# A five-stage audio tower on one core: layernorm applied by ScalarE, and new orders for all engines

## The chip, the core and the metric

The kernel runs on one core of one Trainium2 chip. Its engines run side by side and meet only at semaphores: TensorE (PE in the profile; its weight loads are PEld), VectorE (DVE), ScalarE (ACT), GpSimd (POOL) and SyncE (SP), which here only issues DMAs. The metric is the device time of one launch in microseconds (us), the median of several runs.

## What is computed

The input is 64 sequences of 256 frames of 80 channels. The reference, cut to what matters here:

```python
h = relu(taps5(x) @ W + b)                          # 252 positions of 128 features per sequence
h = batchnorm(h)                                    # statistics over ALL sequences and positions
h = h + attention0(layernorm(h))                    # 8 heads, softmax, band added to the scores
h = h + moe0(layernorm(h))                          # 8 experts of 256, gelu, top 2 of the gates
h = h + linear_attention1(layernorm(h))             # causal, 8 heads, elu + 1
h = h + moe1(attention2(layernorm(layernorm(h))))   # second layernorm has gain and bias; 2 heads, causal;
                                                    # 8 experts of 512, all gates used

def _layernorm(x, axis=-1, eps=1e-05):
    m = jnp.mean(x, axis=axis, keepdims=True)
    v = jnp.var(x, axis=axis, keepdims=True)
    return (x - m) / jnp.sqrt(v + eps)
```

So after the batch norm there are four layernorms per sequence. (The fourth is two in a row, which the kernel folds into one by another variance offset.)

## The kernel before

**Phase 1** (to about 165 us) works on pairs of sequences, 504 positions at a time: `load_x`, a transpose (`turn_input`), the five taps (`taps`), relu on ScalarE, statistics on VectorE, and the result goes to DRAM (`store_y`). Two pairs make a double step k (0 to 15). Beside it the weights arrive in eight pieces of 128 x 1906 float32 (`load_piece`); each is split into a high and a low float16 half by ScalarE (`high_of_piece`) and VectorE (`low_of_piece`). Pieces 0 and 1 come first, piece i+2 in the double step 2i (`PIECE_AT`).

**Phase 2** does everything else for 32 pairs p. Products of float32 values are made from three float16 matmuls (`mm3`: high x high, high x low, low x high). Five kinds of work are written as generators, each cut into steps that end at a `yield`; every engine has its own version of each:

- q, 7 steps: batch norm of pair p, transpose, layernorm, projections of attention 0; their float16 terms go to DRAM and come back spread over partitions (SP's `load_terms`)
- a, 32 steps: attention 0, its output projection, the second layernorm, the gates of the first experts
- l, 48 steps: the third layernorm, linear attention 1, the fourth layernorm, causal attention 2, the gates of the second experts
- h, 48 a round: `hidden`, one chunk of 128 hidden features: PE 3 matmuls of 504 columns into `pf`, ScalarE gelu with bias (L859), VectorE a cast to the high half (L1247), GpSimd the low half (L652)
- o, 48 a round: `output`, one chunk back to 128 features: PE 12 matmuls of 128 columns; at the last chunk of an expert VectorE adds the gated sum to h in four instructions (L1266), and the next expert's first chunk on PE waits for that (`gated`)

The order of the work is written out by hand: one string of 183 letters for each engine and round (`PE_ROUND` and so on), with others for the start and the end. A letter takes the next step of that kind. All engines are in-order, so a step that waits holds up all behind it on its engine. In round r, a belongs to pair r+1, l to pair r, q to pair r+2; the first 28 h belong to the second experts of pair r-1, the next 16 to the first experts of pair r+1.

A layernorm is: `norm_stats` on VectorE (bn_stats L932, bn_aggr L936, variance plus eps L940), `norm` on GpSimd (power -1/2, L584), `norm_apply` on VectorE (L948, four instructions of 126 x 128, minus the mean, times rstd), then `turn` on PE (four transposes, L1327), `high` on ScalarE (L706) and `low` on VectorE (L954).

In the code, PE steps are numbered from 0 in each kind: the layernorm transposes are q5, a24, l2 and l28; the projections of attention 0 are q6 (L1282 to L1284 into pa); its first scores are a0 (L1390, they wait for the spread terms); the logits of the first gates are a25, the transpose of the gates is a29 (L1342) and the product with the output biases a30 (L1348, it waits for ScalarE's copy `gate_t`, L715).

## Time and profile before

| | |
|---|---|
| runs, us | 4356.4, 4362.26, 4363.68 (median 4362.26) |
| profiled execution, us | 4363.7, its span 4362.0 |
| mean granted TensorE clock | 0.982 of 2.4 GHz |
| busy: PE, PEld | 4059.1 us (93%), 2996.2 us (69%) |
| busy: DVE, ACT, POOL | 3341.9 (77%), 2669.0 (61%), 2539.1 (58%) |

PE's busy time is the union of matmuls in flight. A matmul of 128 columns is shown as 0.22 us long but the next one starts 0.06 us later, so PE can lose some time between two that the busy share does not show.

### The profile page before, as it was taken

To read this page: it belongs to the slowest core of one execution; us is meant where nothing else is said; L and a number is where in the kernel's file an instruction comes from. 1 tells how busy PE (TensorE), PEld (TensorE's weight loads), DVE (VectorE), ACT (ScalarE), POOL (GpSimd) and SP (SyncE) were. 2 spreads that over 40 slices of the span, in tenths; PEclk is the share of its full clock that TensorE was granted. 3 is DMA by queue.
4 is the path that set the end of the run, shared out by engine and by line. 5 is a ranking of instruction groups with operands and counts; after the bars stand their busy time and mean duration, and the time that the engine had idled before them with its cause. 6 is when DMAs were issued, how large, how long until landed. Compare 5 with 4: busy or idle time off the path is not lost.

```text
span 4362.0 us, 104576 instructions
## 1 busy us (share of the span) xinstructions
PE 4059.1 (93%) x41344; PEld 2996.2 (69%) x41344; DVE 3341.9 (77%) x9262; ACT 2669.0 (61%) x4345; POOL 2539.1 (58%) x2366
## 2 busy tenths in 40 slices
PE   7678999999999999999999999999999999999998
PEld 3346777776777777677777767777777777777666
DVE  3367777877887777788777778878777887777776
ACT  3235666666666666666666666666666666666654
POOL 2134666666666666666656665665666566666655
PEclk9779999999999999999999999999999999999999
DMA  4200000101100010110001011000101100010000
GB/s 143 72 27 27 20 18 26 30 28 30 30 23 18 23 30 28 30 30 25 20 19 30 28 30 30 28 20 16 30 28 30 30 27 19 18 30 28 28 16 6
DMA packets 136937, 127.60 MB, mean 29 GB/s; under 512 B 28928, under 2 KB 135360, under 8 KB 136448
## 3 DMA queue, kind: packets, MB, share of 16 engines
q1 hardware_dynamic: 136448, 120.91, 9.5%
q8 instruction: 328, 5.37, 0.5%
q14 instruction: 161, 1.32, 0.1%
HBM read 71.05 MB, written 49.55 MB: 28 GB/s over the span
## 4 chain that ended last, share of the span: by engine, by line
PE 53%; DVE 25%; ACT 6%; POOL 5%; issue 4%; DMA 4%; SPq 3%; ACTq 0%; DVEq 0%
PE pf L1282 8%; PE pa L1542 8%; PE pf L1284 7%; PE pf L1283 7%; DVE hid_hi L1247 5%; DVE h L1266 5%; PE pa L1428 3%; PE pa L1524 3%; DMA qk_spread<-terms 3%; PE pa L1414 2%; PE pa L1390 2%; PE pa L1282 2%; PE pa L1622 2%; POOL inv_norm L642 2%; SPq L462 2%
## 5 line engine op out<-in xcount | busy, mean ns | idle before, releaser
L652 POOL TENSOR_TENSOR hid_lo<-hid,hid_hi 128x504 f16<-128x504 f32 x1536 | 1836.6, 1210 | 1363.0 <-DVE hid_hi L1247 1363.0
L859 ACT ACTIVATE hid<-pf,vec 128x504 f32<-128x504 f32 x1536 | 1030.6, 681 | 704.1 <-PE pf L1284 547.1
L1282 PE MATMUL pf<-w_hi,hid_hi 128*126 128x128 f16 x6144 | 1133.4, 224 | 46.0 <-DVE h L1266 45.2
L1284 PE MATMUL pf<-w_hi,hid_lo 128*126 128x128 f16 x6144 | 1119.3, 222 | 0.0
L1283 PE MATMUL pf<-w_lo,hid_hi 128*126 128x128 f16 x6144 | 1119.2, 222 | 0.0
L1282 PEld LDWEIGHTS pf<-w_hi,hid_hi 128*126 128x126 f16 x6144 | 846.6, 138 | 187.0 <-DVE h L1266 88.3
L1283 PEld LDWEIGHTS pf<-w_lo,hid_hi 128*126 128x126 f16 x6144 | 847.5, 138 | 40.3 <-issue 1.4
L1284 PEld LDWEIGHTS pf<-w_hi,hid_lo 128*126 128x126 f16 x6144 | 849.1, 138 | 0.0
L1247 DVE CAST hid_hi<-hid 128x504 f16<-128x504 f32 x1536 | 708.3, 486 | 24.1 <-ACT hid L859 23.9
L1266 DVE SCALAR_TENSOR_TENSOR h<-pf,gates,h 126x128 f32<-126x128 f32 x2048 | 572.8, 341 | 78.0 <-PE pf L1284 77.7
L1282 PE MATMUL pf<-xf_hi,w_hi 128*128 128x504 f16 x1536 | 582.3, 379 | 3.7 <-DVE xf_lo L1229 1.5
L1284 PE MATMUL pf<-xf_hi,w_lo 128*128 128x504 f16 x1536 | 580.8, 378 | 0.0
L1283 PE MATMUL pf<-xf_lo,w_hi 128*128 128x504 f16 x1536 | 580.3, 378 | 0.0
L608 POOL TENSOR_TENSOR pt<-pt,band 126x262 f32<-126x262 f32 x512 | 345.0, 698 | 135.8 <-ACT pt L751 133.8
L1542 PE MATMUL pa<-v,pt 126*126 126x65 f32 x3072 | 382.5, 274 | 1.6 <-DVE o L1147 1.2
L751 ACT ACTIVATE pt<-pa 126x504 f32<-126x504 f32 x512 | 274.5, 588 | 157.6 <-PE pa L1414 156.6
L1542 PEld LDWEIGHTS pa<-v,pt 126*126 126x126 f32 x3072 | 360.9, 191 | 2.1 <-issue 2.1
L1047 DVE TENSOR_REDUCE minus_max<-pa 126x2 f16<-126x504 f32 x512 | 325.9, 682 | 45.8 <-PE pa L1390 44.8
L859 ACT ACT_TABLE_LOAD x248 | 318.2, 1283 | 4.4
L1157 DVE TENSOR_TENSOR pt<-pa,causal 126x504 f32<-126x504 f32 x256 | 173.2, 676 | 151.8 <-PE pa L1524 151.8
L1284 PEld LDWEIGHTS pf<-xf_hi,w_lo 128*128 128x128 f16 x1536 | 150.4, 98 | 179.4 <-issue 4.2
L706 ACT ACTIVATE ot_hi<-pa 128x504 f16<-128x504 f32 x192 | 113.3, 590 | 253.1 <-PE pa L1327 253.0
(206 smaller groups left out, 7390.0 us busy)
## 6 DMA issues: line engine op xcount, KB each, us to landing
qk_spread<-terms SPq DMA_DIRECT2D x224, 126.0 KB, 2.5
qk_spread<-terms SPq DMA_DIRECT2D x192, 63.0 KB, 2.3
y_scratch<-hid SPq DMA_DIRECT2D x32, 252.0 KB, 2.1
y_in<-y_scratch SPq DMA_DIRECT2D x32, 252.0 KB, 3.4
terms<-qk_hi SPq DMA_DIRECT2D x32, 252.0 KB, 2.5
terms<-qk_lo SPq DMA_DIRECT2D x32, 252.0 KB, 2.5
qk_spread<-terms SPq DMA_DIRECT2D x32, 252.0 KB
terms<-ot_hi SPq DMA_DIRECT2D x32, 252.0 KB, 2.4
```

Source lines behind the costliest of these rows:

```text
L608: nc.gpsimd.tensor_tensor(strip, strip, band[0:TILE], ALU.mult).then_inc(S0["p_band"], 1)
L652: nc.gpsimd.tensor_tensor(hid_lo[:, c % 8], hid[:, c % HIDS], hid_hi[:, c % 8], ALU.subtract).then_inc(hid_lo_done[c % 2], 1)
L751: nc.scalar.activation(pt[0][0:TILE, i % 8], pa0[0:TILE, i % 2, 0:TOK], ACT.Exp, scale=HEAD ** -0.5).then_inc(S0["p_exp"], 1)
L859: nc.scalar.activation(hid[:, c % HIDS], pf[:, c % 2, 0:TOK], func, bias=vec[:, bias:bias + 1]).then_inc(F["hid_ready"], 1)
L1047: nc.vector.tensor_reduce(minus_max[0:TILE, 2 * b:2 * b + 2, hd // 2, 64 * (hd % 2) + MAX_ROW], pa0[0:TILE, i % 3, 0:TOK].rearrange("p (t ...
L1157: nc.vector.tensor_tensor(pt[1][0:TILE, i % 4].rearrange("p (t q) -> p t q", t=4), pa1[0:TILE, 0, 0:TOK].rearrange("p (t q) -> p t q", t=4 ...
L1247: nc.vector.tensor_copy(hid_hi[:, c % 8], hid[:, c % HIDS]).then_inc(F["hid_hi_done"], 1)
L1266: last = nc.vector.scalar_tensor_tensor(h[0:TILE, i], pf[0:TILE, 2, i * D:(i + 1) * D], gates[0:TILE, kind, i, e:e + 1], h[0:TILE, i], ALU ...
L1282: nc.tensor.matmul(out, ah, bh, start=start, stop=False, skip_group_check=skip)
L1283: nc.tensor.matmul(out, ah, bl, start=False, stop=False, skip_group_check=skip)
L1284: return nc.tensor.matmul(out, al, bh, start=False, stop=stop, skip_group_check=skip)
L1542: last = nc.tensor.matmul(pa1[0:TILE, 1, first:first + wide], factors[:, cols(blk)], v1[0:TILE, 2 * b + kt, hd], start=(t == 0), stop=(t = ...
```

## The change

Layernorm is no longer applied on VectorE. VectorE writes one more small tile, minus the mean; GpSimd multiplies it by rstd into a `shift`; ScalarE applies `rstd * h + shift` by four activations. The order strings of all engines are others. In phase 1, pieces 2 to 7 now come in the double steps 0 to 5, one in each.

```diff
-PIECE_AT = {2 * i: i + 2 for i in range(EARLY)}
...
-PE_ROUND = ("ohohllhoalhaohhalolhooalholalhhahoaoaohhalholalhaolaalhaoalholloalaalolhaohalhholaohlhaoolhhlaoo"
+PE_ROUND = ("lhhoalhhaoaoloahlohloaoohlhhlaooahlohahalolhalahllaaoolahollhholallhhalaaolaoloahhaolahhlhoohaoo"
...
@@ sync
-            for k in range(PAIRS // 2 - 1):
-                if k in PIECE_AT:
-                    load_piece(PIECE_AT[k])
+            for k in range(EARLY):
+                load_piece(k + 2)
                 load_x(k + 1, 0)
                 store_y(k, 0)
                 load_x(k + 1, 1)
                 store_y(k, 1)
...
@@ gpsimd, norm
                 nc.gpsimd.tensor_tensor(rstd[a][0:TILE], ve[a][0:TILE], minus_half[0:TILE, 0:TILES],
                                         ALU.pow).then_inc(SS[a]["rstd_ready"], 1)
+                pool.wait_ge(SS[a]["rstd_ready"], n(count + 1))
+                nc.gpsimd.tensor_tensor(shift[a][0:TILE], minus_mean[a][0:TILE], rstd[a][0:TILE],
+                                        ALU.mult).then_inc(SS[a]["shift_ready"], 1)
...
@@ scalar
+            def norm_apply(a, count, h, t):
+                S = SS[a]
+                act.wait_ge(S["shift_ready"], n(count + 1))
+                act.wait_ge(S["turned"], n(t))
+                for i in range(TILES):
+                    last = nc.scalar.activation(xn[a][0:TILE, i], h[0:TILE, i], ACT.Identity,
+                                                scale=rstd[a][0:TILE, i:i + 1], bias=shift[a][0:TILE, i:i + 1])
+                last.then_inc(S["xn_ready"], 1)
...
@@ scalar, softmax_attention (and likewise in the q and twice in the l steps)
-                for _ in range(3):
-                    yield
+                yield
+                yield
+                norm_apply(0, p * 2 + 1, ha, p * 3 + 2)
+                yield
                 high(0, p * 3 + 2, xf_hi[:, 0, 0:TOK])
...
@@ vector
+                nc.vector.tensor_scalar(minus_mean[a][0:TILE], mv[a][0:TILE, :, 0], -1.0, 0.0, ALU.mult, ALU.add)
+                scale, offset = (1.0 + EPS, EPS * EPS) if twice else (1.0, EPS)
+                nc.vector.tensor_scalar(ve[a][0:TILE], mv[a][0:TILE, :, 1], scale, offset, ALU.mult,
                                         ALU.add).then_inc(S["var_ready"], 1)
-
-            def norm_apply(a, count, h, t):
-                S = SS[a]
-                dve.wait_ge(S["rstd_ready"], n(count + 1))
-                dve.wait_ge(S["turned"], n(t))
-                for i in range(TILES):
-                    last = nc.vector.tensor_scalar(xn[a][0:TILE, i], h[0:TILE, i], mv[a][0:TILE, i, 0:1],
-                                                   rstd[a][0:TILE, i:i + 1], ALU.subtract, ALU.mult)
-                last.then_inc(S["xn_ready"], 1)
...
-                norm_apply(0, p * 2 + 1, ha, p * 3 + 2)
```

How the orders move is shown at three places of the steady rounds.

**VectorE, from the low halves of the projections of attention 0 (qk_lo, step q6) on.** The first maxima of the scores (minus_max) are step a0 of the next round. Before:

```order
L1026 SCALAR_TENSOR_TENSOR qk_lo<-pa,q_bias,qk_hi 128x504
L1029 SCALAR_TENSOR_TENSOR qk_lo<-pa,vec,qk_hi 128x504
L1034 TENSOR_TENSOR v<-pa,rows 126x8x16 x4
L1247 CAST hid_hi<-hid 128x504
L1266 SCALAR_TENSOR_TENSOR h<-pf,gates,h 126x128 x4
L1006 TENSOR_TENSOR h<-pa,h 126x512
L932 BN_STATS st<-h 126x6 x4
L936 BN_AGGR mv<-st 126x2 x4
L940 TENSOR_SCALAR ve<-mv 126x4
L948 TENSOR_SCALAR xn<-h,mv,rstd 126x128 x4
L1247 CAST hid_hi<-hid 128x504
L1047 TENSOR_REDUCE minus_max<-pa 126x2 x2
```

Now, the last rows up to the same maxima:

```order
L1285 SCALAR_TENSOR_TENSOR h<-pf,gates,h 126x128 x4
L1266 CAST hid_hi<-hid 128x504 x2
L1285 SCALAR_TENSOR_TENSOR h<-pf,gates,h 126x128 x4
L1266 CAST hid_hi<-hid 128x504 x2
L1029 TENSOR_TENSOR h<-pa,h 126x512
L963 BN_STATS st<-h 126x6 x4
L967 BN_AGGR mv<-st 126x2 x4
L970 TENSOR_SCALAR minus_mean<-mv 126x4
L972 TENSOR_SCALAR ve<-mv 126x4
L1069 TENSOR_REDUCE minus_max<-pa 126x2 x2
```

Between qk_lo and the maxima there stood one gated sum (L1266) and two casts of expert work. Now there are three sums and six casts: the eleven rows left out ahead of these, from qk_lo on, hold one sum, two casts, and the logits and the softmax of the second gates. The apply of the third layernorm is gone from VectorE, and nothing waits for the power behind `ve`.

**ScalarE, around the exponentials of the first gates (lge, step a26).** hid is a gelu, xf_hi and xt_hi are high halves after the second and the fourth layernorm's transposes, v is the copy of the last projections, gate_t the transposed gates. Before:

```order
L706 ACTIVATE xf_hi<-pa 128x504
L859 ACTIVATE hid<-pf,vec 128x504 x2
L711 ACT_TABLE_LOAD
L711 ACTIVATE lge<-lg 126x32
L859 ACT_TABLE_LOAD
L859 ACTIVATE hid<-pf,vec 128x504 x2
L706 ACTIVATE xt_hi<-pa,vec 128x504
L859 ACTIVATE hid<-pf,vec 128x504
L811 COPY v<-pa 126x384 x4
L715 COPY gate_t<-pa 128x126
```

Now:

```order
L718 ACTIVATE xf_hi<-pa 128x504
L886 ACTIVATE hid<-pf,vec 128x504 x3
L886 ACT_TABLE_LOAD
L886 ACTIVATE hid<-pf,vec 128x504
L726 ACTIVATE xn<-h,shift,rstd 126x128 x4
L886 ACTIVATE hid<-pf,vec 128x504
L718 ACTIVATE xt_hi<-pa,vec 128x504
L886 ACTIVATE hid<-pf,vec 128x504
L732 ACT_TABLE_LOAD
L732 ACTIVATE lge<-lg 126x32
L838 COPY v<-pa 126x384 x4
L736 COPY gate_t<-pa 128x126
```

The exponentials stood before the first gelu of pair r+1's first experts (h28); now they stand behind its third (h30) and behind xt_hi, and the apply of the fourth layernorm stands between the first and the second.

**PE, from the transpose of the first gates (step a29) on.** Rows into pf are expert work. Before:

```order
L1342 MATMUL pa<-ident,gates 128x126
L1348 MATMUL pa<-b,gate_t 126x128 x4
L1282 MATMUL pf<-w_hi,hid_hi 126x128
L1283 MATMUL pf<-w_lo,hid_hi 126x128
L1284 MATMUL pf<-w_hi,hid_lo 126x128
```

Now, the last rows up to the same product (L1361, the transpose, stands ahead of these, with six rows of the same output chunk between):

```order
L1301 MATMUL pf<-w_hi,hid_hi 126x128
L1302 MATMUL pf<-w_lo,hid_hi 126x128
L1303 MATMUL pf<-w_hi,hid_lo 126x128
L1301 MATMUL pf<-w_hi,hid_hi 126x128
L1302 MATMUL pf<-w_lo,hid_hi 126x128
L1303 MATMUL pf<-w_hi,hid_lo 126x128
L1301 MATMUL pf<-xf_hi,w_hi 128x504
L1302 MATMUL pf<-xf_lo,w_hi 128x504
L1303 MATMUL pf<-xf_hi,w_lo 128x504
L1367 MATMUL pa<-b,gate_t 126x128 x4
```

The product with the biases followed the transpose at once; now one output chunk (12 matmuls) and one hidden chunk (3) stand between them.

## Rows read from the trace of the kernel before

**Rows 1.** Part 1 of the page: busy time of each engine, share of the span, instructions.

```profile
PE 4059.1 (93%) x41344; PEld 2996.2 (69%) x41344; DVE 3341.9 (77%) x9262; ACT 2669.0 (61%) x4345; POOL 2539.1 (58%) x2366
```

**Rows 2.** Windows: stretch, its us, busy us of each engine, granted clock, DMA share, GB/s.

```profile
0.00:170.00 170.00, 131.36 (x612) 63.05 (x612) 61.49 (x79) 54.28 (x74) 23.20 (x30) 0.94 0.42 129
463.00:4000.00 3537.00, 3374.20 (x35427) 2533.07 (x35426) 2840.74 (x7998) 2290.08 (x3732) 2185.97 (x2030) 1.00 0.09 26
```

**Rows 3.** One line of GpSimd, once a pair: ns min/median/max, first and last start.

```profile
L599 POOL TENSOR_TENSOR ha<-ha,rows x32: 1263/1272/1547, 173.8 to 4084.4; 126x512 f32<-126x512 f32 x32
```

**Rows 4.** Waits of PE in 463 to 4000 us: us in total, times, longest us.

```profile
PE pf L1282 <- DVE h L1266: 34.2, 80, 0.7
PE pa L1342 <- DVE gates L1001: 33.9, 28, 1.2
PE pa L1390 <- DMA qk_spread<-terms: 23.8, 27, 2.0
PE pa L1348 <- ACT gate_t L715: 19.8, 56, 0.4
```

**Rows 5.** Groups over the span: busy us, mean ns, idle before and its releaser.

```profile
L948 DVE TENSOR_SCALAR xn<-h,mv,rstd 126x128 f32<-126x128 f32 x256 | 71.4, 343 | 40.7 <-POOL rstd L584 36.8
L706 ACT ACTIVATE xt_hi<-pa,vec 128x504 f16<-128x504 f32 x32 | 24.7, 773 | 1.9 <-PE pa L1327 1.9
L706 ACT ACTIVATE xt_hi<-pa 128x504 f16<-128x504 f32 x32 | 18.9, 591 | 58.1 <-PE pa L1327 58.1
L715 ACT COPY gate_t<-pa 128x126 f32<-128x126 f32 x64 | 16.9, 265 | 78.2 <-PE pa L1342 74.9
L584 POOL TENSOR_TENSOR rstd<-ve,minus_half 126x4 f32<-126x4 f32 x128 | 129.5, 1011 | 68.9 <-DVE ve L940 62.5
L579 POOL TENSOR_TENSOR bn_rstd<-bn_var,minus_half 128x1 f32<-128x1 f32 x1 | 0.6, 555 | 127.4 <-DVE bn_var L918 127.4
L563 POOL MEMSET minus_half<- 128x16 f32 x1 | 0.1, 112 | 0.1
```

**Rows 6.** Timeline, a fourth layernorm on VectorE: start, us, engine, line.

```profile
2124.71 0.68 DVE L1170 TENSOR_TENSOR h<-pa,h 126x512 f32<-126x512 f32 x1
2126.74 0.18 DVE L940 TENSOR_SCALAR ve<-mv 126x4 f32<-126x4 f32 x1
2128.04 1.12 DVE L948 TENSOR_SCALAR xn<-h,mv,rstd 126x128 f32<-126x128 f32 x4
```

**Rows 7.** Timeline, the first gates of one round: PE and DVE, then ACT.

```profile
2002.36 0.65 PE L1327 MATMUL pa<-ident,xn 126*128 126x126 f32 x4
2002.55 1.12 DVE L1266 SCALAR_TENSOR_TENSOR h<-pf,gates,h 126x128 f32<-126x128 f32 x4
2003.72 0.27 PE L1282 MATMUL pf<-w_hi,hid_hi 128*126 128x128 f16 x1 [0.71 <-DVE h L1266]
2005.15 0.38 PE L1282 MATMUL pf<-xf_hi,w_hi 128*128 128x504 f16 x1
2005.36 0.38 PE L1283 MATMUL pf<-xf_lo,w_hi 128*128 128x504 f16 x1
2005.92 0.17 DVE L976 TENSOR_REDUCE lsum<-lge 126x4 f32<-126x32 f32 x1
2011.10 0.33 PE L1342 MATMUL pa<-ident,gates 126*128 126x126 f32 x1 [1.21 <-DVE gates L1001]
...
2000.88 1.28 ACT L859 ACT_TABLE_LOAD   x1
2002.18 1.25 ACT L859 ACTIVATE hid<-pf,vec 128x504 f32<-128x504 f32 x2
2003.32 0.77 ACT L706 ACTIVATE xt_hi<-pa,vec 128x504 f16<-128x504 f32 x1
```

**Rows 8.** Waits of PE in 0 to 463 us.

```profile
PE pf L1295 <- DMA pt<-in_x: 19.5, 15, 3.5
PE pa L1327 <- DVE xn L948: 14.0, 6, 4.5
```

More of the change, by code:

```diff
@@ L298, in program @@
         rstd = [sb(f"rstd{i}", [128, TILES]) for i in range(2)]
+        minus_mean = [sb(f"minus_mean{i}", [128, TILES]) for i in range(2)]
+        shift = [sb(f"shift{i}", [128, TILES]) for i in range(2)]
         lg = [sb(f"lg{i}", [128, TILES, EXPERTS]) for i in range(2)]
@@ L689, in _ @@
             act.wait_ge(small_loaded, 32)
-            for k in range(PAIRS // 2 - 1):
+            for k in range(EARLY):
                 high_of_input(k, 1)
@@ L693, in _ @@
                 high_of_input(k + 1, 0)
-                if k in PIECE_AT:
-                    high_of_piece(PIECE_AT[k])
+                high_of_piece(k + 2)
+                relu(k, 1)
+            for k in range(EARLY, PAIRS // 2 - 1):
+                high_of_input(k, 1)
+                relu(k, 0)
+                high_of_input(k + 1, 0)
                 relu(k, 1)
@@ L725, in softmax_queries_and_keys @@
                 yield
+                norm_apply(0, p * 2, ha, p * 3)
                 yield
@@ L804, in linear_and_causal_attention @@
                     yield
-                for _ in range(3):
-                    yield
+                yield
+                yield
+                norm_apply(1, p * 2 + 1, h1, p * 7 + 5)
+                yield
                 high(1, p * 7 + 5, xt_hi[1][:], vec[:, V_LNG:V_LNG + 1], vec[:, V_LNB:V_LNB + 1])
@@ L894, in _ @@
             low_of_piece(1)
-            for k in range(PAIRS // 2 - 1):
+            for k in range(EARLY):
                 low_of_input(k, 1)
@@ L898, in _ @@
                 low_of_input(k + 1, 0)
-                if k in PIECE_AT:
-                    low_of_piece(PIECE_AT[k])
+                low_of_piece(k + 2)
+                stats(k, 1)
+            for k in range(EARLY, PAIRS // 2 - 1):
+                low_of_input(k, 1)
+                stats(k, 0)
+                low_of_input(k + 1, 0)
                 stats(k, 1)
```

83 lines of the change are left out of this document (42 added, 41 removed).

## The prediction

> **What bounds the kernel now.** I read the page's busy times first: PE 93%, VectorE 77%, ScalarE 61%, GpSimd 58% [rows 1]. Then the windows, to see where PE is not busy. In the steady stretch from 463 to 4000 us PE is busy for 3374 of 3537 us at the full granted clock (1.00, which is 2.4 GHz), and VectorE for 80% of it [rows 2]. The steady rounds take (4084.4 - 173.8) / 31 = 126.1 us each [rows 3], so that stretch holds 28 of them and PE lacks 163 / 28 = 5.8 us a round. Then the waits of PE in the same stretch, which say where [rows 4]: the next expert's first output chunk waits for the gated sum on VectorE (34.2 us, 80 times), the transpose of the first gates for VectorE's top 2 (33.9 us, once a round), the first scores for the DMA that spreads the terms (23.8 us, once a round), the product with the biases for ScalarE's copy (19.8 us, twice a round). No layernorm is among them: the work put between hides all four. PE binds, therefore, and a change can win only in these waits (and in short ones that the busy time hides) or lose by making new ones; 1 us a round is 30 us.
>
> **The engines' balance.** VectorE loses 512 instructions: the half that reads h is busy 71.4 us, the half that reads ha is as large, so -143 us or -4.5 us a round [rows 5]; it gains 128 of 126 x 4, 0.18 us each by the variance row [rows 6], +0.7 us a round. ScalarE gains 16 activations a round of 126 x 128 with a scale and a bias from a tile. The trace has none. A copy of 126 columns takes 265 ns, and scale and bias from a tile make 504 columns 773 - 591 = 182 ns longer [rows 5]: 447 ns, bounds 265 and 773. Activations in a row overlap by 0.11 us (one starts at 2003.32, those before it end at 2003.43 [rows 7]), so four take 4 x 0.447 - 3 x 0.11 = 1.46 us against 1.12 on VectorE [rows 6]. That is +5.8 us a round on ScalarE. Its new order has fewer table loads, 404 against 465 in the program; 61 x 1.28 us [rows 7] = 78 us, 2.6 us a round. Net +3.2 us, and its share goes from some 65% to 67%. GpSimd gains one product of 126 x 4: between 0.11 (a small memset) and 1.01 us (the power of the same size); I take 0.45, under the power of one column at 0.56 [rows 5]. None of these engines becomes the bound.
>
> After the load of a table in this trace the next activation starts at once: 2000.88 + 1.28 = 2002.16, and it starts at 2002.18 [rows 7]. The Trainium skill (ScalarE: Activation LUTs, What ACT_TABLE_LOAD costs) says that a switch costs a drain of some 1.38 us more, 2.66 us in all; by that rule, which the row doesn't show, ScalarE would be freed of 162 instead of 78 us. ScalarE isn't the bound, so the sum would not move.
>
> **The chain of a layernorm.** In the fourth one the path from the residual add to the end of the apply takes 2129.16 - 2124.71 = 4.45 us [rows 6]. Now: +0.1 for the extra tile ahead of the variance (up to 0.18), +0.5 for the product and its semaphore (0.15 to 1.1), +0.34 for the slower apply (-0.4, with 265 ns each, to +1.6, with 773): 5.4 us, bounds 4.3 to 7.3. What hides it is the work that PE's order puts in between. A hidden chunk costs PE 3 x 0.213 = 0.64 us (2005.15 to 2005.36 is one matmul), an output chunk 0.70 (24 matmuls from 2003.72 to 2005.15 are two) [rows 7]. Adding up the orders, the fourth layernorm has 5.2 us of PE work in front of its transposes before and 5.8 now; the third 5.0 and 6.6; the second 8.5 and 7.9; the first 21 and 15. So the first three are hidden, and the fourth is just hidden (5.4 of 5.8). I charge 0.1 us a round: +3 us. On ScalarE each apply stands behind gelus whose chunk PE has finished before the shift is there (for the second: h23 ends 3.2 us after the projection, the shift is ready after 4.0), so little queues behind a waiting apply.
>
> **Parts of the new orders**, each by the same count over 30 rounds:
>
> - Spread terms. From the projections of attention 0 to the first scores PE has 6.6 us of work before and 9.8 now. The wait is 0.88 us in the mean and 2.0 at most [rows 4], less than the 3.2 us won: all 25 us go. Below: none if SP's stores come later, above: 25.
> - Bias product. After the first gates' transpose 1.3 us of PE work now precedes the product; after the second gates' still none. Half of 19.8 us goes: -10.
> - First gates. VectorE needs 2011.10 - 2005.92 = 5.2 us from the first sum to PE's transpose, and this starts 2.9 us after the fourth layernorm's transposes end (2003.01) [rows 7]. Now the exponentials wait for the gelu of h30: PE ends that chunk 0.64 us behind the transposes, the gelu ends at about 1.5, the table load at 2.8, the exponentials (some 0.25, as the copy of 126 columns [rows 5]) at 3.1. The first sum starts 0.3 us later than before; PE's work up to the transpose is the same (5.5 us). +9.
> - Gated sums. Between experts PE has 16 borders a round. The work of other kinds on them is 43 us before and 57 now; the four shortest are 0.6, 0.8, 1.2, 1.2 before and 1.1, 1.2, 1.3, 1.3 now. The sum on VectorE takes 1.12 us (from 2002.55; the matmul at 2003.72 waited for it [rows 7]); against a need of 1.4 they lack 1.8 us before and 0.7 now. I cut 34.2 us [rows 4] in that proportion: -21, bounds 0 and -36.
> - Places made tighter: the two halves of attention 2's scores have 0.6 us between them instead of 2.0, the second and third maxima of attention 0 have 0.7 instead of 2.0. 0.4 us a round: +12, bounds 0 and +30.
>
> **The start.** Before the experts begin, the layernorms of the first pairs have nothing beside them: PE waited 14.0 us there, 6 times [rows 8]. Each gets longer by 0.94, and four waits that were just hidden come to light: +10. The weight pieces cost a wait for x behind each 953 KB piece, whichever double step they stand in (19.5 us in all, at most 3.5 [rows 8]); six still come. I take 0, bounds -5 and +15, since six in a row leave PE idle more densely and its granted clock in phase 1 is 0.94 already [rows 2].
>
> **Sum.** -25 - 10 + 9 - 21 + 12 + 3 + 10 = -22 us. The profiled execution took 4363.7 us, 1.4 above the median of the runs: 4341.7 against it, so I say 4342.
>
> **Rivals.**
>
> 1. *The waits only change place, no change.* The order before had also been laid so that its waits were short, and 5.8 us a round were left all the same. My counts see the four waits of before and not those that the new order will make, on VectorE's and ScalarE's queues. For it: 56 waits of 0.35 us are no more than a semaphore's way [rows 4]. Against it: VectorE, on which 68 of the 112 us of [rows 4] wait, has 3.8 us less to do. Time: 4355 to 4370, say 4362.
> 2. *The layernorm's chain comes out on the path: slower.* Place: the transposes of the fourth and the third layernorm. If the product costs as much as the power (1.01) and the apply 0.6 us apiece, the chain is 4.45 + 0.1 + 1.1 + 1.0 = 6.7 us. It decides from 5.8 us (fourth) and about 6.2 (third, whose need is larger by the last gated sum and smaller by the add). 0.9 + 0.5 us a round = +42; gelus queue behind the waiting apply on ScalarE and PE's hidden chunks behind these, as much again at worst. With -22 - 3 of the rest: 4381 to 4425, say 4390. For it: the margin is 0.4 us by my own numbers. Against it: 0.447 comes from two direct rows.
> 3. *VectorE's relief goes further.* All waits for gated sums go (-36 instead of -21), the gates' transpose comes 0.5 us sooner because casts don't stand ahead of it (-15 instead of +9), and no place gets tighter: 4363.7 - 25 - 10 - 15 - 36 + 3 + 10 = 4291. For it: VectorE waited 36.8 us for the power in front of the apply with a full queue behind [rows 5]; those stalls end.
>
> **How the numbers follow.** Forecast 0.42 (4310 to 4355), rival 1 0.18, rival 2 0.25, rival 3 0.15. The range 4290 to 4395 cuts off about half of rival 3's low side and the upper third of rival 2. 0.2% is 8.7 us, about what a measurement of this kernel tells from no change. Faster: the forecast and rival 3, 0.57; same 0.18; slower 0.25.
>
> **What would show it.** In the steady stretch of the changed kernel: no wait of PE's first scores for the spread DMA; the bias product waits 28 times instead of 56; the first gates' transpose waits 1.2 to 1.6 us once a round; no wait of the layernorms' transposes for ScalarE (rival 2 if there is one of over 0.3 us a round); the activations into xn near 0.45 us, the product on GpSimd near 0.45; rounds of 125.3 us; 403 to 404 table loads. Phase 1 ends within 5 us of before. I would be wrong in the main if new waits, of ScalarE for the shift or of PE for casts, add up to over 0.7 us a round.

## The result, and the profile after

The changed kernel takes 4320.7 us (median of 5 runs, 4314.27 to 4337.08) against 4362.26: ratio 0.9914, 95% interval 0.9899 to 0.9928. The forecast was 4342, the range 4290 to 4395. The direction and the range hold. The sum was 21 us short, and one of its terms had the wrong sign.

Part 1 of the page after:

```profile
PE 4066.8 (94%) x41344; PEld 3009.8 (70%) x41344; DVE 3367.6 (78%) x8878; ACT 2784.5 (64%) x4796; POOL 2596.6 (60%) x2494
```

The two windows of [rows 2] after:

```profile
0.00:170.00 170.00, 130.82 (x612) 63.29 (x612) 62.30 (x79) 53.63 (x73) 24.94 (x30) 0.94 0.43 129
459.00:3996.00 3537.00, 3423.27 (x35900) 2580.27 (x35899) 2902.35 (x7754) 2416.67 (x4169) 2266.90 (x2172) 1.00 0.09 26
```

The GpSimd line of [rows 3] after:

```profile
L607 POOL TENSOR_TENSOR ha<-ha,rows x32: 1266/1460/1467, 175.5 to 4056.3; 126x512 f32<-126x512 f32 x32
```

PE lacks 114 us in 3537 where it lacked 163 [rows 2]. Part 1 holds a surprise: VectorE has 384 instructions fewer and is busy 26 us *longer* [rows 1]. Where the time went, by PE's own hidden chunks (one fixed chunk of a round in each trace): the second round starts at 529.02 us before and 529.45 after, the 29 rounds behind it take 126.96 and 125.48 us each, the end 151.1 and 150.7. (The 126.1 us of the prediction is the spacing of [rows 3], which also spans the first and the last pairs; on that scale it is 125.2 now.) So the start costs 0.4 us by then (1.6 at the first round), the end gives 0.4, and all the rest, 29 x 1.48 = 43 us, is in the steady rounds.

The waits of PE in the steady stretch, after (us in total, times, longest), to be laid beside [rows 4]:

```profile
PE pa L1630 <- ACT fs L861: 21.5, 28, 0.8
PE pa L1346 <- ACT xn L726: 19.3, 28, 0.7
PE pa L1614 <- ACT pt L843: 17.2, 28, 0.6
PE pa L1301 <- DVE xt_lo L1199: 10.0, 28, 0.4
PE pa L1367 <- ACT gate_t L736: 9.9, 28, 0.4
PE pa L1422 <- DVE qk_spread L1075: 9.5, 28, 0.3
PE pa L1543 <- DMA qk_spread<-terms: 8.8, 13, 1.1
PE pa L1603 <- DVE v L1215: 5.1, 28, 0.2
```

They add up to 101 us. Before, the same view had the 112 us of [rows 4] and 39 more that rows 4 don't show, 150 in all. These are not all small: the transposes of attention 2's weights (L1611 before, L1630 now) waited 20.6 us for `o` and 8.3 for `fs`, more than the product with the biases, and now wait 21.5 for `fs`. The difference of 49 us is the difference of PE's idle time. Of the four entries of [rows 4], three are gone (gated sums 34.2, first gates 33.9, first scores' DMA 23.8) and the fourth is halved (19.8 to 9.9). In their place stand the fourth layernorm (19.3, and 10.0 for the half behind it) and attention 2's scores (17.2).

Why does the first gates' transpose not wait any more? The timeline of before around it, VectorE and GpSimd (start, us, engine, line):

```profile
2008.79 0.42 DVE L999 TENSOR_REDUCE lge<-ob 126x32 f32<-126x256 f32 x1
2009.24 1.80 DVE L1001 SCALAR_TENSOR_TENSOR gates<-lge,lg 126x32 f32<-126x32 f32 x1
2010.97 0.41 DVE L1247 CAST hid_hi<-hid 128x504 f16<-128x504 f32 x1
...
2009.10 1.89 POOL L638 TENSOR_TENSOR o<-v 126x1024 f32<-126x1024 f32 x1 [2.11 <-ACT v L811]
```

An instruction on 32 columns takes 1.80 us. It starts 0.14 us after GpSimd's squares of q and k and ends 0.05 us after they end (2009.10 + 1.89 = 2010.99). The same place after:

```profile
2123.56 0.19 DVE L1024 SCALAR_TENSOR_TENSOR gates<-lge,lg 126x32 f32<-126x32 f32 x1
2123.67 0.42 DVE L1266 CAST hid_hi<-hid 128x504 f16<-128x504 f32 x1
...
2123.85 1.99 POOL L646 TENSOR_TENSOR o<-v 126x1024 f32<-126x1024 f32 x1 [3.64 <-ACT v L838]
```

The squares start 0.29 us after the gates, and the gates take 0.19 us. The wait that I had priced as VectorE's work looks like a collision with GpSimd (two runs below test it), and the new orders happen to separate the two. But they bring others together. The gates before, then the gates, the product of v, the low half after the fourth layernorm (xt_lo) and the gated sum after (ns minimum, median, maximum, first and last start):

```profile
L1001 DVE SCALAR_TENSOR_TENSOR gates<-lge,lg x32: 192/1795/1799, 243.9 to 4170.4; 126x32 f32<-126x32 f32 x32
```

```profile
L1024 DVE SCALAR_TENSOR_TENSOR gates<-lge,lg x32: 191/191/193, 246.2 to 4130.4; 126x32 f32<-126x32 f32 x32
L1215 DVE TENSOR_TENSOR v<-v,inv_norm x32: 1224/2153/2156, 372.7 to 4245.7; 126x1024 f32<-126x1024 f32 x32
L1199 DVE TENSOR_TENSOR xt_lo<-fs,xt_hi x32: 683/1279/1283, 362.6 to 4235.5; 128x504 f16<-128x504 f32 x32
L1285 DVE SCALAR_TENSOR_TENSOR h<-pf,gates,h x2048: 331/342/352, 251.6 to 4315.9; 126x128 f32<-126x128 f32 x187
```

The product of v lasts 2.15 us now (its group had a mean of 1225 ns before), since it meets GpSimd's hid_lo. So does xt_lo, in nearly every round: hid_lo starts 0.40 us ahead of it and it takes 1279 ns instead of 683. The 0.6 us are more than the 0.36 us a round that PE waits for it (10.0 us above). The gated sum L1285, which takes one input from PSUM, never lasts longer: 331 to 352 ns in 2048 instructions, 1446 of which start while GpSimd works. The casts to hid_hi are held most, here before and after as groups (busy us, mean ns):

```profile
L1247 DVE CAST hid_hi<-hid 128x504 f16<-128x504 f32 x1536 | 708.3, 486 | 24.1 <-ACT hid L859 23.9
```

```profile
L1266 DVE CAST hid_hi<-hid 128x504 f16<-128x504 f32 x1536 | 845.4, 573 | 8.2 <-ACT hid L886 2.7
```

I summed, over all VectorE instructions, the time above the median duration of their operation and shape: 181 us before, 322 after. How large that sum is depends on what is taken as undisturbed. Without such a choice: the instructions that both kernels have last 124 us longer in sum after the change (casts to hid_hi +134, product of v +28, xt_lo +14, gates -48). That is most of why VectorE's busy time didn't fall.

The Trainium skill (SBUF — State Buffer, section "SBUF: two separate sides") says that VectorE and GpSimd share a pair of ports as an exclusive lock: whoever starts first has it for the whole instruction, if VectorE's runs in a 2-port mode or has two SBUF inputs while GpSimd's reads SBUF, and "the other fully blocks". The trace agrees for the gates: 1.80 us instead of 0.19, with the squares already running. It doesn't agree for GpSimd's powers: 185 casts start while one runs, with up to 2.2 us of it left, and all take 0.41 to 0.42 us.

### The profile page after: what moved, and what is told of

The parts are those of the page before. It is cut to its first block, busy times and chain, and to the rows that moved or that the text cites. A ratio compares the mean times of both kernels' runs of the same rounds, so it can differ in the third digit from the quotient of the medians.

```text
span 4319.1 us, 104773 instructions
## 1 busy us (share of the span) xinstructions
PE 4066.8 (94%) x41344; PEld 3009.8 (70%) x41344; DVE 3367.6 (78%) x8878; ACT 2784.5 (64%) x4796; POOL 2596.6 (60%) x2494
## 4 chain that ended last, share of the span: by engine, by line
PE 56%; DVE 24%; ACT 6%; POOL 5%; issue 4%; DMA 3%; SPq 2%; ACTq 0%; DVEq 0%; POOLq 0%
PE pf L1301 9%; PE pf L1303 8%; PE pf L1302 8%; PE pa L1561 8%; DVE h L1285 4%; PE pa L1447 3%; DVE hid_hi L1266 3%; PE pa L1543 3%; PE pa L1346 2%; PE pa L1433 2%; POOL inv_norm L650 2%; PE pa L1301 2%; ACT xn L726 2%; PE pa L1641 2%; PE pa L1303 2%
## 5 line engine op out<-in xcount | busy, mean ns | idle before, releaser
L660 POOL TENSOR_TENSOR hid_lo<-hid,hid_hi 128x504 f16<-128x504 f32 x1536 | 1835.5, 1212 | 775.8 <-DVE hid_hi L1266 775.8
L886 ACT ACTIVATE hid<-pf,vec 128x504 f32<-128x504 f32 x1536 | 1014.7, 680 | 505.5 <-PE pf L1303 356.9
L1301 PE MATMUL pf<-w_hi,hid_hi 128*126 128x128 f16 x6144 | 1133.7, 224 | 10.7 <-DVE h L1285 10.2
L1266 DVE CAST hid_hi<-hid 128x504 f16<-128x504 f32 x1536 | 845.4, 573 | 8.2 <-ACT hid L886 2.7
L1285 DVE SCALAR_TENSOR_TENSOR h<-pf,gates,h 126x128 f32<-126x128 f32 x2048 | 574.1, 342 | 155.2 <-PE pf L1303 152.6
L616 POOL TENSOR_TENSOR pt<-pt,band 126x262 f32<-126x262 f32 x512 | 351.2, 707 | 527.6 <-ACT pt L773 527.4
L1301 PEld LDWEIGHTS pf<-xf_hi,w_hi 128*128 128x128 f16 x1536 | 152.7, 99 | 125.0 <-issue 41.2
```

The lines of the kernel that those rows point to most:

```text
L616: nc.gpsimd.tensor_tensor(strip, strip, band[0:TILE], ALU.mult).then_inc(S0["p_band"], 1)
L660: nc.gpsimd.tensor_tensor(hid_lo[:, c % 8], hid[:, c % HIDS], hid_hi[:, c % 8], ALU.subtract).then_inc(hid_lo_done[c % 2], 1)
L886: nc.scalar.activation(hid[:, c % HIDS], pf[:, c % 2, 0:TOK], func, bias=vec[:, bias:bias + 1]).then_inc(F["hid_ready"], 1)
L1266: nc.vector.tensor_copy(hid_hi[:, c % 8], hid[:, c % HIDS]).then_inc(F["hid_hi_done"], 1)
L1285: last = nc.vector.scalar_tensor_tensor(h[0:TILE, i], pf[0:TILE, 2, i * D:(i + 1) * D], gates[0:TILE, kind, i, e:e + 1], h[0:TILE, i], ALU ...
L1301: nc.tensor.matmul(out, ah, bh, start=start, stop=False, skip_group_check=skip)
```

## The experiments

Theory 1: the gain lies in the places of the new orders. Theory 2: it lies in VectorE's relief. The kernel before was timed again beside each run, with medians of 4356 to 4361 us; all ratios are to it. The last column is worked out from the trace as above.

| run | us | ratio, 95% interval | us a round |
|---|---|---|---|
| before / the change | 4362.3 / 4320.7 | 0.9914 (0.9899 to 0.9928) | 126.96 / 125.48 |
| old_orders | 4570.8 | 1.0476 (1.0459 to 1.0492) | 133.8 |
| orders_only | 4641.6 | 1.0637 (1.0620 to 1.0654) | 135.7 |
| squares_late | 4340.2 | 0.9951 (0.9937 to 0.9965) | 126.19 |
| pieces_old | 4326.0 | 0.9915 (0.9900 to 0.9930) | |
| old_orders_placed | 4381.1 | 1.0044 (1.0031 to 1.0056) | 127.14 |
| new_orders_dve | 4434.7 | 1.0176 (1.0162 to 1.0190) | 129.06 |
| squares_in_four | 4337.8 | 0.9952 (0.9939 to 0.9964) | 126.21 |
| one_chunk_and_wait | 4561.1 | 1.0465 (1.0450 to 1.0479) | 133.56 |
| dve_ballast | 4439.2 | 1.0188 (1.0174 to 1.0202) | 129.26 |
| shift_four | 4368.6 | 1.0027 (1.0016 to 1.0038) | 126.85 |
| hid_lo_halves | 4377.5 | 1.0043 (1.0029 to 1.0057) | 127.12 |
| variance_first | 4312.7 | 0.9904 (0.9888 to 0.9921) | 125.14 |

### Is the gates' wait a collision? Two runs on the kernel before

*squares_late.*

```diff
                 pool.wait_ge(S1["qkv_ready"], n(p * 4 + 4))
+                if 1 <= p < PAIRS - 1:
+                    pool.wait_ge(S0["gate_ready"], n(p + 2))
                 nc.gpsimd.tensor_tensor(squares[0:TILE], ...
```

> The kernel before with one wait more: from pair 1 on GpSimd's squares (1.89 us, L638) wait until VectorE has written the gates (L1001). Theory 1 (VectorE's last gates instruction is held while GpSimd runs its squares, so that it takes 1.80 us where the changed kernel has 0.19): it falls to 0.2 us, the gates' transpose on PE loses most of its 34 us of waits, and the time falls by 15 to 35 us, to 4327 to 4347. Rival (the instruction is slow by itself or by its place, or PE waits next for what the squares feed): it stays at 1.7 us, or the time stays within 10 us of 4362.

*squares_in_four.*

```diff
-                nc.gpsimd.tensor_tensor(squares[0:TILE], qkv[0:TILE, :, 0:2 * D], qkv[0:TILE, :, 0:2 * D],
-                                        ALU.mult).then_inc(S1["sq_ready"], 1)
+                for i in range(TILES):
+                    last = nc.gpsimd.tensor_tensor(squares[0:TILE, i], qkv[0:TILE, i, 0:2 * D],
+                                                   qkv[0:TILE, i, 0:2 * D], ALU.mult)
+                last.then_inc(S1["sq_ready"], 1)
```

> The kernel before, with GpSimd's squares of q and k (126x1024, 1.89 us) made in four instructions of 126x256, the order unchanged. Theory 1 (a VectorE instruction that collides with one of GpSimd is held to the end of that GpSimd instruction): the gates instruction on VectorE falls from a median of 1.80 us to between 0.2 and 0.7 us (the remainder of one short instruction), PE's wait for gates falls from 33.9 us to below 15, and the time by 10 to 20 us: 4342 to 4352 us, ratio 0.9955 to 0.9977. Theory 2 (the two share a path and slow each other while both run, or VectorE waits for the whole run of GpSimd's work): the gates instruction still takes 1.2 us or more and the time stays within 5 us of before (0.999 to 1.001).

The gates' line in the first and in the second:

```profile
L1003 DVE SCALAR_TENSOR_TENSOR gates<-lge,lg x32: 191/192/194, 245.6 to 4148.6; 126x32 f32<-126x32 f32 x32
```

```profile
L1003 DVE SCALAR_TENSOR_TENSOR gates<-lge,lg x32: 193/516/521, 242.7 to 4146.4; 126x32 f32<-126x32 f32 x32
```

Without the meeting it takes 192 ns; with instructions a quarter as long it is held for a quarter's remainder (it ends 0.05 us after that quarter), though GpSimd's total work is not smaller. In both, PE's wait for gates is gone from the list and the time falls by 21 and 22 us. That is not the full 34: waits of 21.6 and 23.0 us for the product of v came in, which the kernel before did not have. The theory "held to the end of the other instruction" is shown; "the two slow each other while both run" falls. The second run gained a little more than the 10 to 20 us expected. Both runs are on the kernel before; that the same 21 us are part of the change's 42 is inferred.

### One half of the change alone

*old_orders:* the changed code with the orders of before, ScalarE's apply steps moved by a gelu.

```diff
-ACT_ROUND = ("lhaaohahloaalhlolhhholhahlolahhoalahooaallllooaoahohlllhhhooolaolloaallaahohaalhoalhhhlahaoalhao"
+ACT_ROUND = ("aoohohaollhlhhaooollhhlaooholoaooahhlhahhallolhaaalaooalolaohallhlaalhaalaohhhhoallahlhaalhlhool"
...
```

> The changed code (layernorm applied by ScalarE, shift on GpSimd, pieces in the first double steps) with the orders of before; only ScalarE's four apply steps a pair, empty before, are placed where they cannot deadlock, behind the gelu that is one ahead of the cast at which VectorE applied. Theory 1 (the gain lies in which waits the new orders remove, above all the gates' transpose, and the move by itself costs): PE still waits some 30 us for the gates and 24 us for the spread DMA, and the layernorm's transposes begin to wait for ScalarE; 4365 to 4400 us. Theory 2 (the gain is VectorE's relief): 4320 to 4340 us even in the old orders.

4571 us, 94 us of PE waiting for xn and 88 for ot_lo (which the next expectation calls ot_hi): the apply stood too early on ScalarE, waited up to 4.1 us for the shift, and held up what stood behind it. A miss of the expectation, and no test of the theory. The same with these steps later:

```diff
-... hhhhoallahlhaalhlhoolohahhoaalhohoqllaolohlaaaoo ...
+... hhhhoallahlhalhlahoolohahhoaalhollhoqaolohlaaaoo ...
```

> The changed code (ScalarE applies the layernorm, GpSimd makes the shift) with every order string of the kernel before, except that ScalarE's four apply steps stand two to four gelus later, as far behind the statistics as in the changed kernel's own order. In the run before this one they stood too early, and it took 4571 us with 94 us of PE waiting for the second layernorm and 88 us for ot_hi. Theory 1 (the gain lies in the places: VectorE is not held by GpSimd at the gates, the gated sums and the bias product find their operands; who applies the layernorm is worth nothing in itself): GpSimd's squares and VectorE's gates again overlap, the gates instruction takes about 1.8 us and PE waits about 34 us for gates over the rounds; the time is 4350 to 4395 us, the ratio 0.997 to 1.008. Theory 2 (the gain comes from VectorE's relief of 3.8 us a round): 4310 to 4335 us, ratio below 0.995, with orders of before. Rival: the apply on ScalarE needs its new orders, since PE's waits for xn stay above 50 us: above 4400 us.

4381, inside theory 1's range, but for another reason than I gave. The gates are *not* held here (191 ns), since with the changed steps of ScalarE the copies of v come later and GpSimd's squares with them; that should have given 20 us. Waits for the layernorms took it and more (PE's waits in the steady stretch, here and below):

```profile
PE pa L1342 <- ACT xn L722: 55.6, 31, 2.0
PE pa L1626 <- DVE o L1219: 20.9, 28, 0.8
PE pa L1363 <- ACT gate_t L732: 19.9, 56, 0.4
PE pa L1405 <- DMA qk_spread<-terms: 18.9, 27, 1.6
```

VectorE is busy for 3170 us there, 172 less than before, and it is worth nothing: theory 2 alone falls.

*orders_only:* the code of before with the new orders, VectorE applying in the steps that are empty in the new order.

```diff
-PE_ROUND = ("ohohllhoalhaohhalolhooalholalhhahoaoaohhalholhalaolaalhaoalholloalaalolhaohalhholaohlhaoolhhlaoo"
+PE_ROUND = ("lhhoalhhaoaoloahlohloaoohlhhlaooahlahohalolhalahllaaoolahollhholallhhalaaolaoloahhaolahhlhoohaoo"
...
```

> The kernel before with all the new orders, but layernorm applied by VectorE and the pieces where they were. Theory 1: at most 15 us from the changed kernel, 4305 to 4335 us, with no wait of PE for the gates' transpose. Theory 2: VectorE has 3.8 us more a round and its waits come back, 4345 to 4370 us.

4642 us, outside both ranges: 155 us of PE waiting for xn. The apply came right behind the statistics, where VectorE had to wait for the power (29 us of waits listed in the steady rounds) and held up what stood behind it; how the 155 us come from that I did not follow further. With the apply one or two casts later:

```diff
-... laohalohhoalooohloalllhhoahoahohal ... holhhooolhoalhlaaohqhholhollao ...
+... laohaolhhoalooohloalllhhoahoahohal ... holahhooolhoalhlaaohqlhhohollao ...
```

> The code of before (VectorE applies the layernorm, ScalarE's and GpSimd's apply and shift steps do nothing) in the changed kernel's orders, with VectorE's four apply steps moved behind the statistics, so that VectorE doesn't stand waiting as it did in the run before this one (4642 us, 155 us of PE waiting for the second layernorm). Theory 1 (the places carry the gain): 4318 to 4350 us, ratio 0.990 to 0.998; the gates instruction on VectorE takes about 0.19 us as in the changed kernel and PE's layernorm transposes wait 0 to 1 us a round. Theory 2 (moving the apply off VectorE carries it): 4355 us or more, ratio 0.998 or above, with waits of PE for VectorE's casts of ot or of the gated sums, 1 to 2 us a round more than in the changed kernel.

4435, which theory 2's case (4355 or more) covers, with waits of the kind it names: 26.4 us for gated sums and 28.0 for ot_lo that the changed kernel doesn't have. PE's wait for xn is 37.0 us against 19.3. So the new orders alone don't carry the gain either: theory 1 alone falls too. The apply takes 430 to 541 ns an instruction there against 339 to 343 in the kernel before, held by GpSimd, and VectorE's instructions are held for 444 us in all.

### Load on VectorE, or the chain?

*dve_ballast:* the changed kernel; the layernorm chain is untouched.

```diff
+            def ballast(a):
+                for i in range(TILES):
+                    nc.vector.tensor_scalar(spare[0:TILE, a, i], ident[0:TILE], bn_scale[0:TILE, 0:1],
+                                            bn_shift[0:TILE, 0:1], ALU.subtract, ALU.mult)
...
                 norm_stats(0, p * 2, ha)
                 yield
+                ballast(0)
                 yield
```

> The changed kernel, with four VectorE instructions of the shape of the old apply (126x128) added at the four places of a round where VectorE applied the layernorm, on spare data and with no wait: load on VectorE alone, about 3.8 us a round, nothing of the layernorm chain. The new orders with the apply on VectorE took 4435 us, 114 us above the changed kernel. Theory A (in the new orders VectorE's load decides; the apply had to leave it): the time is 4370 to 4435 us, ratio to before 1.002 to 1.017, with PE waiting for VectorE's h, ot_lo or qk_spread 1 to 3 us more a round. Theory B (the 114 us came from the layernorm chain and its waits, xn and ot_lo, and the load itself finds gaps): 4318 to 4340 us, ratio 0.990 to 0.995.

4439, the same as with the real apply on VectorE and 4 us above theory A's range. Most of the waits that grow end at VectorE, though not at the gated sums (none is listed):

```profile
PE pa L1311 <- DVE ot_lo L983: 35.4, 28, 1.3
PE pa L1311 <- DVE xt_lo L1209: 32.8, 28, 1.2
PE pa L1356 <- ACT xn L727: 26.5, 28, 1.0
PE pa L1640 <- ACT fs L862: 20.8, 27, 0.8
PE pa L1419 <- DVE minus_max L1076: 18.2, 54, 0.4
```

The group of the added instructions (busy us, mean ns, idle before):

```profile
L978 DVE TENSOR_SCALAR spare<-ident,bn_scale,bn_shift 126x128 f32<-126x128 f32 x512 | 180.5, 414 | 0.0
```

180 us of load, 5.6 us a round where 3.8 were meant, cost 118 us. Theory A is shown: in these orders VectorE has no room for the apply, and nothing of the chain is needed to explain the 114 us. "Load" includes the collisions that it brings: the mean cast to hid_hi is 610 ns here against 573.

*hid_lo_halves:* fewer or shorter holds, on the changed kernel.

```diff
+                    for part in (slice(0, TOK // 2), slice(TOK // 2, TOK)):
+                        last = nc.gpsimd.tensor_tensor(hid_lo[:, c % 8, part], hid[:, c % HIDS, part],
+                                                       hid_hi[:, c % 8, part], ALU.subtract)
+                    last.then_inc(hid_lo_done[c % 2], 1)
```

> The changed kernel with GpSimd's hid_lo (128x504, about 1.2 us) made in two instructions of 128x252. In the changed kernel VectorE's instructions last in sum 322 us longer than in their undisturbed form (181 us before the change), 248 us of it at the cast to hid_hi, nearly all while GpSimd runs hid_lo. If such an instruction is held to the end of the GpSimd instruction that it meets, the hold halves: the cast's mean falls from 573 to about 500 ns and VectorE's busy time by 80 to 130 us. What that is worth: if VectorE's load decides (114 us for 3.8 us a round, from the run with the apply left on VectorE), 0.3 to 1 us a round, 4290 to 4312 us; if the casts find their gaps anyway, within 5 us of 4321; if GpSimd's own fixed cost (0.1 to 0.2 us more for each of 48 chunks a round) makes it late, above 4330.

The hold falls, by less than half: the cast's mean goes from 573 to 521 ns and VectorE's busy time down by 80 us, the low end of what was expected. And the time rises by 57 us, as in the third case. GpSimd pays: two halves take 2 x 710 ns against 1212, 252 us in the program, and PE now waits for it. PE also waits for the maxima on VectorE, and why isn't shown:

```profile
PE pa L1348 <- ACT xn L728: 30.8, 28, 1.1
PE pf L1303 <- POOL hid_lo L661: 27.4, 28, 1.0
PE pa L1411 <- DVE minus_max L1071: 21.1, 71, 0.5
```

### The layernorm's chain

*shift_four* (the changed kernel).

```diff
+                for i in range(4):
+                    last = nc.gpsimd.tensor_tensor(shifts[a][0:TILE, i], minus_mean[a][0:TILE], rstd[a][0:TILE],
+                                                   ALU.mult)
+                last.then_inc(SS[a]["shift_ready"], 1)
```

> The changed kernel with GpSimd's product for the shift (0.23 us) made four times for each layernorm, the last one used: the chain from the statistics to PE's transposes is 0.6 to 0.7 us longer at each of the four layernorms of a round. If the fourth layernorm's chain is on the path in the changed kernel (PE waits 0.69 us there once a round) and the other three have slack of 0.7 us or more: PE's wait for xn grows from 19 to 35-40 us and the time by 15 to 20 us, to 4336 to 4341 us (ratio 0.994 to 0.9955). If that wait of 0.69 us only took the place of another one a little later: under 6 us more. If more layernorms have no slack: 30 us or more (above 4350).

PE's wait for xn in the steady stretch:

```profile
PE pa L1349 <- ACT xn L729: 51.7, 84, 1.3
```

The time is 48 us more, not 15 to 20 (41 us between the two profiled executions). The wait comes 84 times in 28 rounds instead of 28: three of the four layernorms have less than 0.65 us of slack. Taken apart by layernorm, the fourth waits 17.4 us more (0.62 us a round), which is what was expected of it, the third 10.2 us where it had none (0.37 a round), the second 4.8 (0.17 a round). The first still doesn't wait.

*variance_first* (the changed kernel; GpSimd waits once more, ahead of the shift).

```diff
-                nc.vector.tensor_scalar(minus_mean[a][0:TILE], mv[a][0:TILE, :, 0], -1.0, 0.0, ALU.mult, ALU.add)
                 scale, offset = (1.0 + EPS, EPS * EPS) if twice else (1.0, EPS)
                 nc.vector.tensor_scalar(ve[a][0:TILE], mv[a][0:TILE, :, 1], scale, offset, ALU.mult,
                                         ALU.add).then_inc(S["var_ready"], 1)
+                nc.vector.tensor_scalar(minus_mean[a][0:TILE], mv[a][0:TILE, :, 0], -1.0, 0.0, ALU.mult,
+                                        ALU.add).then_inc(S["var_ready"], 1)
```

> The changed kernel with VectorE's two small instructions behind the statistics exchanged: the variance with eps, for which GpSimd's power waits, is made first, and minus_mean second, while the power runs (GpSimd waits for it before the shift). The layernorm chain gets 0.08 to 0.1 us shorter at each of the four layernorms. The run with the shift made four times lengthened it by 0.65 us and cost 48 us, 7 us for 0.1 us. If that slope holds in the other direction: 4313 to 4317 us, ratio to before 0.9890 to 0.9905, with PE's wait for xn at 16 to 18 us in place of 19.3. If the extra wait on GpSimd takes back what is gained, or the slope holds only upwards: within 3 us of the changed kernel (4318 to 4324).

4312.7, and rounds of 125.14 us instead of 125.48. PE's wait for xn falls from 19.3 to 10.3 us, further than the 16 to 18 expected, and 6.6 of these 9 come back as a wait for xt_lo:

```profile
PE pa L1303 <- DVE xt_lo L1201: 16.6, 29, 0.6
PE pa L1348 <- ACT xn L727: 10.3, 29, 0.4
```

The mechanism isn't that of the expectation. In the fourth layernorm the chain gets 0.33 us shorter, not 0.1, since the power takes 1.01 us there instead of 1.28 (GpSimd in one round, to be laid beside the timeline further down); why it does stays open:

```profile
2107.36 1.01 POOL L589 TENSOR_TENSOR rstd<-ve,minus_half 126x4 f32<-126x4 f32 x1
```

The wait for xt_lo grows by a collision once more: xt_lo comes earlier, meets more of the same hid_lo and takes 1491 ns (median) where it took 1279.

It has the lowest median of the study, at the lower edge of what the slope gave. That is luck: the slope was applied to 0.1 us, and the chain moved by three times that. And its interval overlaps that of the change, so that it beats the change is likely and not shown.

### Two more

*pieces_old:* the changed kernel with the weight pieces in every other double step.

```diff
+PIECE_AT = {2 * i: i + 2 for i in range(EARLY)}
...
-            for k in range(EARLY):
-                load_piece(k + 2)
...
+            for k in range(PAIRS // 2 - 1):
+                if k in PIECE_AT:
+                    load_piece(PIECE_AT[k])
```

> The changed kernel with the weight pieces in every second of the first double steps, as before. Both theories: no effect, within 4 us of the changed kernel's 4320.7, phase 1 as long to within 2 us. A rival, that six pieces in a row let PE's clock sink: 5 to 10 us faster.

The same ratio (the median is 5.3 us above 4320.7, a little more than expected, but the kernel before took 4361.2 beside it), and the granted clock to 170 us is 0.94 in both: the pieces' new places are worth nothing that can be measured.

*one_chunk_and_wait:* the changed kernel, meant to beat it.

```diff
-... holhalhloqlolhlolollhhlooqlhhqololhh ...
+... holhaolhloqlolhlolollhhlooqlhhqlolhh ...
...
                                         ALU.pow).then_inc(S1["rn_ready"], 1)
+                pool.wait_ge(S1["qkn_ready"], n(p + 1))
```

> The changed kernel with two edits. One output chunk of PE's round order stands ahead of attention 2's first scores instead of behind them (PE waits there 0.6 us a round for ScalarE's pt), and GpSimd, after its second power, waits until VectorE has multiplied v by inv_norm before it goes on (that product took 2.15 us in the changed kernel against 1.23 us before, since it overlapped a GpSimd instruction). If waits that end at such a hold are worth their time: the product is back at 1.23 us in most pairs, the wait of PE for pt (17.2 us) is below 5 and that for v (5.1 us) near none, the time 4298 to 4315 us, ratio to before 0.985 to 0.989. If VectorE and ScalarE are only late a little further on: within 5 us of 4321, ratio 0.989 to 0.992, with the same waits under other names. If GpSimd is late from its new wait: above 4325, with PE or VectorE waiting for GpSimd's hid_lo or shift.

4561. The product of v is back at 1226 ns and the waits for pt and v are gone, as the expectation's first case says, and 240 us are lost elsewhere:

```profile
PE pf L1301 <- DVE h L1285: 161.1, 134, 2.5
PE pf L1301 <- POOL hid_lo L660: 36.1, 27, 1.3
```

The third case (above 4325, PE waiting for hid_lo) is there with 36 us: GpSimd's hid_lo now stands 40 us behind its new wait for the product of v. It doesn't cover the larger part. Which of the two edits makes the 161 us of waits for gated sums stays open; they were not run apart.

## Why the prediction was right or wrong

- **PE binds, and only its waits count.** Right: the sum of listed waits fell by 49 us and PE's idle time with it. The rounds got 1.48 us shorter where the forecast had 0.8 (126.1 to 125.3; 126.1 to 125.2 by the same spacing of [rows 3], which shows the drop too small). But "in these waits" left out 39 us of others, among them the 28.9 us at L1611, which shrank by 7 unforeseen.
- **Spread terms, -25.** Right for the first scores (23.8 to none). A wait of 8.8 us for the terms of linear attention (L1543) is new and was not seen: -15 net.
- **Bias product, -10.** Right: 28 waits instead of 56, 9.9 us left.
- **First gates, +9.** Wrong, measured -34. The step that failed is "VectorE needs 5.2 us from the first sum to PE's transpose", taken as fixed work and carried over. 1.6 us of it were the hold by GpSimd's squares. The median of one small instruction (1795 ns, where a neighbour that reads as many columns took 0.17 us [rows 7]) would have told it.
- **Gated sums, -21, bounds 0 and -36.** Gone altogether, -34; the proportion was too timid. The share of rival 3 that rests on this came true.
- **Tighter places, +12.** Near: attention 2's scores wait 17.2 us, new. The maxima of attention 0 don't show, so all of it is at the first of the two places.
- **The fourth layernorm, +3.** Too small: 19.3 us for its transposes. The 10.0 for the low half behind are no part of the chain that I summed; they come with the collision of xt_lo and hid_lo. The timeline after:

```profile
2110.72 0.77 DVE L1266 CAST hid_hi<-hid 128x504 f16<-128x504 f32 x1
2111.41 0.68 DVE L1190 TENSOR_TENSOR h<-pa,h 126x512 f32<-126x512 f32 x1
2113.52 0.16 DVE L972 TENSOR_SCALAR ve<-mv 126x4 f32<-126x4 f32 x1
...
2113.76 1.28 POOL L589 TENSOR_TENSOR rstd<-ve,minus_half 126x4 f32<-126x4 f32 x1 [0.17 <-DVE ve L972]
2115.12 0.27 POOL L592 TENSOR_TENSOR shift<-minus_mean,rstd 126x4 f32<-126x4 f32 x1
...
2115.43 1.65 ACT L726 ACTIVATE xn<-h,shift,rstd 126x128 f32<-126x128 f32 x4 [0.89 <-POOL shift L592]
...
2117.13 0.65 PE L1346 MATMUL pa<-ident,xn 126*128 126x126 f32 x4 [0.69 <-ACT xn L726]
```

  From the residual add to the end of the apply it is 2117.08 - 2111.41 = 5.67 us, where I had 5.4: the four applies 1.65 instead of 1.46, the power with the product +0.61 instead of +0.5 (the product 0.27, but the power 1.28 where I had left it at 1.01). That is under the 5.8 of the filler, and PE waits all the same. The add stands behind a cast that is held (0.77 us instead of 0.41), which may be the reason; no run tests it. Rival 2's mechanism is there, at a wait of 0.69 us a round, over its own threshold of 0.3; its total isn't. shift_four shows how close it was: 0.65 us more of chain and the kernel is slower than before. "The first three are hidden" was true, but for the third and the second with less than 0.65 us to spare, where I had counted 0.8 us for the third (6.2 - 5.4, rival 2) and 2.5 for the second (7.9 - 5.4). "Little queues behind a waiting apply" on ScalarE was wrong: it waits 92 us for the shift in the steady rounds, 3.3 us a round. By my own sign (new waits of ScalarE for the shift over 0.7 us a round) I would be wrong in the main. The sign was a bad one, since ScalarE isn't the bound and PE gets 0.69 us a round of it.
- **The start, +10.** Measured +1.6 at the first round, +0.4 at the second. PE's waits for xn there are 12.8 us, against 14.0 [rows 8]. The product took 0.20 to 0.28 us, not 0.45, and the added time didn't come to light.
- **Weight pieces, 0.** Right. Phase 1 has the same clock and busy time [rows 2].
- **The engines' balance.** ScalarE and the table loads came as worked out (68% of the steady stretch against my 67, 404 loads). VectorE did not: -143 + 27 us of instructions became +26. 124 us of that are instructions that last longer, the other 18 overlap lost between neighbours. So "VectorE's relief" as less busy time was the wrong picture, though dve_ballast shows that the new orders need the room. The two halves of the change need each other: alone, in the placings I tried, they cost +21 and +74 us, together they give -42.
- **Luck in the sum.** The terms missed by more than the 21 us: some 73 us too high (gates 43, gated sums 13, start 10, L1611 7) and some 46 too low (the fourth layernorm with xt_lo 26, terms of linear attention 10, tighter places 5, product of v 5). That the range holds is in part these misses cancelling.
- **What stays open.** The gates' share (21 us) was moved by itself, on the kernel before. The shares of the spread terms and the gated sums are read from PE's waits; no run moves one of them alone.

Of the rivals, the first (waits change place) holds for 60 of the 109 us of waits that went or shrank, which came back under other names; the second is real and small; the third has the gated sums and the gates right, the collision behind the latter unseen, and "no place gets tighter" wrong.

## What to carry to other kernels

Where an instruction's median is many times that of others of its shape, look at what runs beside it before counting it as work: here 1.6 of 1.8 us of "VectorE" were GpSimd's, worth 21 us to whoever moved or shortened the GpSimd instruction. When work is moved off an engine, look at the sum of instructions and the sum of holds apart; the busy share mixes them. And a hand-made order fits the engine that it was made for: test a move of work and its order together, and price the slack of each chain by lengthening it on purpose.

## What the hardware showed that I had not expected

- A VectorE instruction that starts while one of GpSimd's squares, hid_lo or band instructions (pt, L616) runs is held until that one is over, if its inputs are in SBUF and it is a cast, a tensor_scalar or takes two tiles: 0.19 to 1.80 us for the gates, 1.22 to 2.15 for the product of v, 0.68 to 1.28 for xt_lo, 0.41 to 1.42 at most for the casts. It doesn't end with the other. It ends later by its own length less some 0.14 us, in the median 0.05 us later for the gates, 0.28 for the casts, 0.54 for xt_lo, 1.08 for the product of v. With an operand from PSUM (L1285) no hold is seen.
- Not every instruction of GpSimd holds: beside a power (L589, L650) no VectorE instruction of the changed kernel lasts over 0.03 us longer, neither the casts nor an instruction on two SBUF tiles (lg, L993, 30 times with 1.04 us of the power left).
- GpSimd's instructions get longer too: the power 1157 ns against 1011 [rows 5], the add of L607 1460 against 1272 [rows 3], and a hid_lo that starts while VectorE multiplies v takes 2.12 us instead of 1.14.
- GpSimd's product of 126 x 4 takes 234 ns in the mean and the power of the same size 1157 (the rows below): the operation, not the size, makes the power dear.
- Splitting a GpSimd instruction of 504 columns in two costs 208 ns more in all (2 x 710 against 1212).

```profile
L592 POOL TENSOR_TENSOR shift<-minus_mean,rstd 126x4 f32<-126x4 f32 x128 | 30.0, 234 | 10.0
L589 POOL TENSOR_TENSOR rstd<-ve,minus_half 126x4 f32<-126x4 f32 x128 | 148.1, 1157 | 134.2 <-DVE ve L972 134.2
```
